# Post-norm transformer layer on one core: five shared places for probabilities, products with V in fewer and longer blocks, one more step of the softmax sums on TensorE

## What is computed

```python
qkv = encodings @ W_attn + b_attn
scores = jnp.einsum('bhki,bhqi->bhkq', k, q) / math.sqrt(HEAD)
scores = jnp.where(mask, scores, jnp.float32(-10000.0))
attn = jax.nn.softmax(scores, axis=2)
combined = jnp.einsum('bhkq,bhkl->bhql', attn, v)
x = _layernorm(x + out @ W_out + b_out)
top_scores, top_idx = jax.lax.top_k(hidden_states @ w_router, k)
h = jax.nn.gelu(selected @ W1 + b1); processed = h @ W2 + b2
x = _layernorm(x.at[top_idx].add(sigmoid(top_scores) * processed))
```

## Time and profile before

| | |
|---|---|
| median of 3 runs (lowest, highest) | 2496.51 us (2496.45, 2498.16) |
| profiled execution, its own time | 2497.64 us |
| its span | 2495.8 us |
| mean granted TensorE clock | 0.993 |
| PE busy | 2437.9 us (98%) |
| POOL busy | 1566.2 us (63%), nearly all of it in the attention part |

### The profile page before, as it was taken

One profiled execution on the slowest core, in us unless ns is written; L12 is line 12 of the kernel. 1 busy time (PEld: TensorE's weight loads), 2 busy tenths in 40 slices (PEclk: granted clock), 3 DMA queues, 4 the chain that ended last, 5 costly groups with the idle time before them and its releaser, 6 DMA issues.

```text
span 2495.8 us, 40908 instructions
## 1 busy us (share of the span) xinstructions
PE 2437.9 (98%) x14104; PEld 1798.0 (72%) x14104; DVE 1677.7 (67%) x4384; ACT 1227.0 (49%) x2211; POOL 1566.2 (63%) x1481
## 2 busy tenths in 40 slices
PE   8999999999999999999999999998999999999997
PEld 6666676777677767676767667763788888888886
DVE  6767778778777777777888787775755544553533
ACT  3665566666566666666666666666531111111110
POOL 2877888788877888877888888885323132221311
PEclk9999999999999999999999999998999999999999
DMA  4233445335344444534434354343421011010100
GB/s 178 95 128 117 161 138 199 129 124 187 136 146 162 145 145 141 175 133 166 157 129 161 125 180 145 128 162 97 169 64 43 19 34 33 26 34 26 32 20 17
DMA packets 167649, 287.72 MB, mean 115 GB/s; under 512 B 23258, under 2 KB 58138, under 8 KB 166172
## 3 DMA queue, kind: packets, MB, share of 16 engines
q1 hardware_dynamic: 160276, 268.26, 31.1%
q0 software_dynamic: 7168, 16.85, 2.1%
HBM read 117.23 MB, written 65.11 MB: 73 GB/s over the span
## 4 chain that ended last, share of the span: by engine, by line
PE 83%; POOL 11%; DVE 2%; issue 1%; ACT 1%; DMA 0%; SPq 0%; POOLq 0%; DVEq 0%; ACTq 0%
PE PS L1623 14%; PE PS L1602 14%; PE PS L1464 11%; POOL Pa L902 10%; PE PS L1549 10%; PE PS L1515 9%; PE PS L1567 9%; PE PS L1472 8%; PE PS L1477 6%; PE PS L1484 2%; POOL Pm L858 1%; PE PS L1439 1%; PE PS L1583 0%; DVE nm L1130 0%; DVE xTl L1223 0%
## 5 line engine op out<-in xcount | busy, mean ns | idle before, releaser
L902 POOL TENSOR_TENSOR Pa<-Pa,Pm 128x512 f32<-128x512 f32 (+1 forms) x602 | 751.9, 1271 | 129.3 <-ACT Pm L1012 106.7
L1549 PE MATMUL PS<-Qp,Kp 128*128 128x512 f32 (+3 forms) x1536 | 491.0, 355 | 8.7 <-ACT Pm L1012 4.1
L1515 PE MATMUL PS<-Kp,Qp 128*128 128x512 f32 (+3 forms) x1536 | 485.3, 351 | 6.6 <-DVE nm L1130 5.5
L1012 ACT ACTIVATE Pm<-PS 128x512 f32<-128x512 f32 (+1 forms) x643 | 358.3, 568 | 243.7 <-PE PS L1549 194.0
L1130 DVE TENSOR_REDUCE nm<-PS 128x1 f32<-128x512 f32 x512 | 344.7, 687 | 157.2 <-PE PS L1515 156.9
L902 POOL TENSOR_TENSOR Pa<-Pa,P 128x512 f32<-128x512 f32 (+1 forms) x297 | 371.9, 1274 | 64.7 <-ACT P L1012 53.6
L1515 PEld LDWEIGHTS PS<-Kp,Qp 128*128 128x128 f32 x1536 | 276.2, 189 | 105.4 <-issue 41.6
L974 ACT ACTIVATE G<-PS,b1c 128x512 f32<-128x512 f32 x128 | 88.2, 689 | 536.5 <-PE PS L1602 520.3
L1549 PEld LDWEIGHTS PS<-Qp,Kp 128*128 128x128 f32 x1536 | 274.8, 189 | 93.5 <-ACT Pa L1012 29.0
L1138 DVE CUSTOM_DVE_ANT_0 PS<-PS,maskA 128x384 f32<-128x384 f32 (+3 forms) x512 | 246.3, 509 | 121.9 <-PE PS L1515 119.9
L1623 PE MATMUL PS<-W2h,Gs 128*128 128x512 f32 x1024 | 316.6, 390 | 1.1 <-DVE W2l L1228 1.1
(11 more groups left out here) (154 smaller groups left out, 4261.2 us busy)
## 6 DMA issues: line engine op xcount, KB each, us to landing
Qp<-nat SPq DMA_DIRECT2D x192, 256.0 KB, 2.5
Kp<-nat SPq DMA_DIRECT2D x192, 256.0 KB, 2.9
o_s<-Of SPq DMA_DIRECT2D x64, 256.0 KB, 2.1
xb<-in_x SPq DMA_DIRECT2D x64, 256.0 KB, 3.4
Ot<-o_s SPq DMA_DIRECT2D x64, 256.0 KB, 3.0
h_s<-hs SPq DMA_DIRECT2D x64, 256.0 KB, 2.1
out<-xb SPq DMA_DIRECT2D x64, 256.0 KB, 2.2
x_raw<-in_xt SPq DMA_DIRECT2D x15, 1024.0 KB, 6.4
```

The lines of the kernel that those rows point to most:

```text
L902: e.tensor_tensor(to, to, probs(u, k)[:, h0:h0 + many, 0:w], ALU.add).then_inc(s["padd"], many)
L1012: e.activation(probs(u, k)[:, hh[0]:hh[-1] + 1, 0:w], tile_bank(j)[:, 0:len(hh) * w].rearrange("p (h n) -> p h n", n=w), ACT.Exp).then_inc ...
L1515: ins = e.matmul(to, Qp[:, u % 4, h_, qt * P:qt * P + P], Kp[:, (2 * i + k0 // 512) % 4, h_, 0:w], start=True, stop=True)
L1549: ins = e.matmul(tile_bank(j)[:, x_ * w:x_ * w + w], Kp[:, (2 * i + k // 4) % 4, h_, k % 4 * P:k % 4 * P + P], Qp[:, u % 4, h_, 512 - w:51 ...
```

## The change

It does four things.

1. The steps of a unit are multiplied with V in fewer blocks: the even unit's four steps in one, the odd unit's eight in 0-1, 2-3 and 4-7.
2. N of the even unit stands behind the odd unit's block 0-1, N of the odd one behind its block 4-7, in the same run of 32-column matmuls. F then stands alone between 128-column matmuls.
3. The last two steps of an odd unit (256 and 128 wide) are summed on PE; POOL makes two additions (of two heads each) less in each of 31 odd units.
4. All five buffers of probabilities (a to e) are one set whose roles turn from pair to pair. The place of a step says which step's reader the exponential waits for. The order of POOL's `keep` and additions comes from a small planner (`sums`) with a cost for each.

```diff
-PRODUCTS = (((0,), (1, 2, 3)), ((0,), (1, 2), (3, 4), (5, 6, 7)))
-PV_LAG = ((1, 2), (2, 2, 3, 3))
+PRODUCTS = (((0, 1, 2, 3),), ((0, 1), (2, 3), (4, 5, 6, 7)))
+PV_LAG = 2
+IN_SUMS = 2
+PLACES = "abccdebcaebb"
+TURN = {"a": "c", "b": "a", "c": "e", "d": "d", "e": "b"}
+KEEP_BEATS, ADD_BEATS, EXP_BEATS = 0.39, {512: 0.78, 384: 0.62, 256: 0.78, 128: 0.78}, 0.6
...
-    return u % 2 == 1 and k == ksteps(u) - 1
+    return u % 2 == 1 and k >= ksteps(u) - IN_SUMS
...
+    steps = [(x_, y_) for x_ in range(max(0, u - 3), u + 1) for y_ in range(ksteps(x_)) if (x_, y_) < (u, k)]
+    last = [x_ for x_ in steps if place_of(*x_) == place_of(u, k)][-1:]
...
-        return 15
+        return 14
...
-                n = self.formed[u, k1] + PV_LAG[u % 2][j]
+                n = self.formed[u, k1] + PV_LAG
+                if u % 2 and j != 1 and not by_products(u):
+                    n = max(n, self.beat["N", u - 1 if j == 0 else u])
...
+    def sums(self):
...
+                if (u, k) not in keeps:
+                    at_add = max(self.formed[u, k] + EXP_BEATS, self.multiplied[u, 0] + 1)
+            t = max(t, min(at_keep, at_add))
+            if at_keep <= t:
+                self.adding.setdefault(int(t), []).append((keeps.pop(0), None))
+                t += KEEP_BEATS
+            else:
+                self.adding.setdefault(int(t), []).append(((u, k), h0))
+                pieces.pop(0)
+                t += ADD_BEATS[width(u, k)]
...
                         e.wait_ge(s["padd"], 4 * additions(a))
                         if k == 1:
                             e.wait_ge(s["pv"], ksteps_before(u) + 1)
...
+                        for u0, k0 in occupants(u, k):
+                            if by_products(u0) and k0 < ksteps(u0) - 1:
...
+                        for k_ in range(ksteps(u)):
+                            if in_sums(u, k_):
+                                ins = sums(u, k_)
...
-                todo += [(1, 2, x_) for x_ in T.pieces[n] if x_[0][0] == "N"]
+                todo += [(3, 2, x_) for x_ in T.pieces[n] if x_[0][0] == "N"]
```

More of the change, by code:

```diff
@@ L98, in in_sums, with place_of, occupants, many_heads @@
 def in_sums(u, k):
-    return u % 2 == 1 and k == ksteps(u) - 1
+    return u % 2 == 1 and k >= ksteps(u) - IN_SUMS
 def additions(a):
-    return a - a // 10
+    return (10 - IN_SUMS) * (a // 10) + min(a % 10, 10 - IN_SUMS)
+def place_of(u, k):
+    name = PLACES[4 * (u % 2) + k]
+    for _ in range(u // 2):
+        name = TURN[name]
+    return name
+def occupants(u, k):
+    if k == ksteps(u) - 1:
+        return []
+    steps = [(x_, y_) for x_ in range(max(0, u - 3), u + 1) for y_ in range(ksteps(x_)) if (x_, y_) < (u, k)]
+    last = [x_ for x_ in steps if place_of(*x_) == place_of(u, k)][-1:]
+    return [x_ for x_ in steps if last and x_[0] == last[0][0] and place_of(*x_) == place_of(u, k)
+            and (x_ == last[0] or x_[1] == last[0][1] - 1 == ksteps(x_[0]) - 2)]
+def many_heads(w):
+    return 1 if w > 256 else 2 if w > P else HG
 def by_products(u):
@@ L206, in __init__ @@
         self.streams()
+        self.sums()
         self.nat, self.packs, self.freed = {}, {}, {}
@@ L251, in streams @@
     def streams(self):
-        self.tiles, self.formed, self.products = {}, {}, {}
+        self.tiles, self.formed, self.products, self.multiplied = {}, {}, {}, {}
         ring = []
@@ L283, in streams @@
             self.ring_no[x[:3]] = j
+    def sums(self):
+        self.adding = {}
+        keeps = [(u, k) for u in range(U) for k in range(ksteps(u)) if diag(u, k) is not None]
+        pieces = [(u, k, h0) for u in range(U) for k in range(1, ksteps(u)) if not by_products(u) and not in_sums(u, k)
+                  for h0 in range(0, HG, many_heads(width(u, k)))]
+        t = float(self.first)
+        while keeps or pieces:
+            at_keep = self.formed[keeps[0]] + EXP_BEATS + (2 if keeps[0][1] == 0 else 0) if keeps else 1e9
+            at_add = 1e9
+            if pieces:
+                u, k, h0 = pieces[0]
+                if (u, k) not in keeps:
[8 more added lines that the diff above has]
+                t += ADD_BEATS[width(u, k)]
     def vector_in(self, n):
@@ L880, in gpsimd @@
                         layer_norm(o_number(j))
-                for u, k in T.steps_formed(n):
-                    i = diag(u, k)
-                    if i is not None and not kept_early(u, k):
+                for (u, k), h0 in T.adding.get(n, ()):
+                    if h0 is None:
                         keep(u, k)
[L885 to L888, removed]
+                        continue
+                    a, w = added(u, k), width(u, k)
+                    if h0 == 0:
+                        if diag(u, k) is not None:
+                            e.wait_ge(s["keep"], diag(u, k) + 1)
                         else:
@@ L893, in gpsimd @@
                             e.wait_ge(s["pv"], ksteps_before(u) + 1)
[L894 to L903, removed]
+                    many = many_heads(w)
+                    to = probs(u, 0)[:, h0:h0 + many, 512 - w:512]
+                    e.tensor_tensor(to, to, probs(u, k)[:, h0:h0 + many, 0:w], ALU.add).then_inc(s["padd"], many)
                 for j in o_add.get(n, ()):
```

34 lines of the change are left out of this document (11 added, 23 removed).

## The result

The changed kernel takes 2621.85 us (median of 4 executions, 2619.41 to 2623.04), the kernel before 2496.73 (2496.45 to 2498.16): a ratio of 1.0496, 95% interval 1.0484 to 1.0509, or 125 us slower. The prediction was 2574, in a range of 2500 to 2625.

The account below looks back on a forecast made before the run. PE's own work was taken as the bound, with waits for POOL coming in. 49 us (middle) + 3 (first pairs) + 25 (clock) = 77 on the profiled 2497.64, which stands 1.13 above the median: 2574 us, range 2500 to 2625.

Parts of the forecast that it names:

- The mechanism: At the odd unit's S step of 512, PE waits for POOL's late-started additions in every pair; chance 0.62.
- The size of the wait in the middle: PE waits for POOL from f + 23.4 to f + 25.5, 2.1 us in every pair; mean 2.4 us.
- None of the four `keep` is late: In POOL's odd-unit chain, exponentials of step 5 are over by about f + 11.4; their `keep` comes at f + 11.2.
- 2.1 - 0.22 = +1.9: Middle pairs without DVE's split: a 2.1 us wait for POOL, less 0.22 us of PE's own work.
- The first pairs: First four pairs, without output projection: both kernels wait for POOL, PE's part is 5 us shorter; +3 us (0 to +8).
- The end: The last unit pair, summed without POOL, was left at zero, give or take 5 us.
- The clock: Waits of PE lower the clock in half of the 30 pairs: 15 x 1.7 = 25 us, ends 0 and 50.
- PE's own work: On PE, 62 fewer blocks save 20.5 us, S steps of 256 cost 13.5: -7 us, -0.22 a pair.
- F alone: F standing alone 62 times on PE, not heading a block: difference taken as zero (-3 to +3 us).
- counting mode changes: By the skill's drain rule on PE, lone F counts too: nothing of 20.5 us saved, work grows by 13.5; prediction rejected it.
- The other waits: Exponentials on ACT wait for readers of shared places: costed at nothing, at most 8 us.
- The old waits: PE's waits of 0.31 and 0.59 us in one pair of four go: about 0.3 us a pair.

Follow-up runs that it names:

- fifth experiment: Changed kernel with N of the odd unit back behind F and the two 384 tiles, V steps 4 to 7 in their own block ahead of F: 2602.95 us.
- third experiment: Changed kernel with each `keep` of POOL planned 0.8 beat later: 2595.53 us.
- the filler: Changed kernel with nine dummy matmuls of 512 ahead of PE's wait at N of the odd unit, from unit 5 on: 2615.7 us.
- second experiment: Changed kernel with the last three steps of each odd unit summed on PE, not two (`IN_SUMS = 3`): 2538.82 us.
- last experiment: Kernel before with the five turning places alone, POOL's order and everything else as before: 2497.52 us.
- seventh experiment: Kernel before with only the odd unit's S step of 256 summed on PE too: 2500.61 us.
- the eleventh and the twelfth kernel: Kernel before with turning places and planner, bias additions at the change's beats: 2505.69 us; with turning places alone, POOL's order as before: 2497.52 us.

## Why the prediction was right in direction and short by 48 us

**The mechanism: right.** V step 0 in the block ahead of F makes POOL start late, and PE waits at the S step of 512. The runs pulled at both ends of the wait: V step 0 earlier gives 86 us, a shorter chain 83, and a chain 0.70 us shorter 0.69 in the half where it stands. It also holds that N's own place hardly matters ("The period is POOL's chain plus PE's way from N to the next V step 0"): the fifth experiment shows it, and in its expectation I had forgotten my own sentence.

**The size of the wait in the middle: short by some 20 us.** With f for the time of the even unit's F, as in the prediction: start, forecast f - 2.4, measured f - 2.24. The additions end: forecast f + 25.5, measured f + 26.31. N could have gone out at f + 23.4 by the forecast, at f + 23.78 by the trace (1078.41 less the wait of 2.59). So the wait is 2.59 and not 2.1. The failed term is "None of the four `keep` is late": two are, by 0.93 and 0.54 us, and without those gaps the chain is 0.70 us shorter (third experiment). I had laid out PE's order by hand for the exponentials of these steps, and PE reaches their B tiles later than that (ACT waits there for most of them, up to 1.53 us). The pairs without DVE's split stood in the sum at 2.1 - 0.22 = +1.9 and came out at +2.7: 0.5 is the wait, 0.3 PE's own part (such a pair takes 52.79 us without its wait, and took 52.70 before). That is 16 us in 20 pairs; the pairs with the split came out as forecast (+2.0), and 4 us are those named above.

**The first pairs: wrong, some 16 us.** "Both kernels wait for POOL there" was a claim that no row bore, and of the kernel before it is true for 2.6 us only. PE's waits for POOL at N in the first four of these pairs, before and after:

```profile
PE PS L1484 <- POOL Pa L902: 2.6, 4, 0.7
```

```profile
PE PS L1519 <- POOL Pa L944: 16.3, 4, 4.3
```

Before, POOL started early enough that 0.7 us was the longest wait. With the late start a PE whose way is 5 us shorter waits all the longer, some 4 us a pair. Of the +28.5 up to the eleventh F some 9 are the clock, 14 this wait, and 5 are PE's waits for DVE's maxima (9.8 us, before 4.7), where I took 3 in all without the clock.

**The end: wrong, some 9 us.** I left it "at zero, give or take 5". Most of it isn't the pair summed without POOL but the last chain with it: some 7 of the 9 us lie in the half of that chain. POOL's timeline after, at the last odd unit that POOL sums (its F at 1786.4):

```profile
1788.36 0.19 POOL L915 TENSOR_SCALAR lnrs<-lnmv 128x1 f32<-128x1 f32 x1 [7.31 <-DVE lnmv L1373]
...
1789.95 5.02 POOL L944 TENSOR_TENSOR Pa<-Pa 128x512 f32<-128x512 f32 x4
```

and before (its F at 1673.7):

```profile
1668.38 10.83 POOL L902 TENSOR_TENSOR Pa<-Pa,Pm 128x512 f32<-128x512 f32 x8 [3.98 <-ACT Pm L1012]
1679.30 0.19 POOL L867 TENSOR_SCALAR lnrs<-lnmv 128x1 f32<-128x1 f32 x1
```

The chain's new place is behind a layer norm's scalars, and those wait for DVE. It starts 3.5 us after F, not 5.3 ahead of it, and PE waits 6.15 us. What is queued ahead of a moved instruction must be looked up at the ends of the program too, where the pattern of the middle doesn't hold.

**The clock: right in sum.** Forecast 15 falls of 1.7, 25 us. There were 21 more than before, and the filler shows 1.3 us for one (one profile of each): 27 us, 14 of them in the middle. The share of the middle's waits with a fall was near the forecast half: 10 of the 25 waits for POOL had one, and the eleventh fall stands behind the 3.35 us for DVE. The Trainium skill (TensorE: Matmul & The Clock Gate, Why this matters for your kernels) ties the loss to gaps longer than these waits; the row at 909.12 disagrees, the one at 1078.41 doesn't.

In all: 21 + 16 + 9 + 2 for the clock are the 48 us. That the range still holds the time, by 3 us, is luck in part: the room in it was meant for the clock, which came as forecast, while the first pairs (19 for 0 to 8) and the end (9 for 5 at most) left their own bounds.

**PE's own work: nearly right, with two terms off that nearly cancel.** In the second experiment, where PE hardly waits, pairs without DVE's split take 53.30 us from F to F where the ones before take 52.74. Two S steps more (0.43 and 0.65) and the 0.31 below would make +1.39, and it is +0.56: two blocks fewer and two lone F give back 0.83 us where I had 0.66. F alone costs next to nothing: it goes out at 1052.04 and the next matmul at 1052.07. By the Trainium skill (TensorEngine Tiling (Array Packing), Key Properties) each change of mode drains TensorE; the trace shows 0.1 us at either end of a run of 32-column steps and next to nothing for this 16-column transpose, so counting mode changes would have been wrong here, as the prediction held.
Against it stands a wait that I hadn't seen. With N ahead of the two 384 tiles, ACT does N's logarithm and exponential first and the exponentials of those tiles later. ACT's timeline after, then PE's:

```profile
1137.16 0.58 ACT L1082 ACTIVATE PS<-PS 128x512 f32<-128x512 f32 x1 [3.71 <-PE PS L1474]
1137.78 0.58 ACT L1084 ACTIVATE PS<-PS 128x512 f32<-128x512 f32 x1
1138.27 0.87 ACT L1047 ACTIVATE P<-PS 128x384 f32<-128x384 f32 x2
```

```profile
1137.98 0.68 PE L1499 MATMUL PS<-xTh,Wkh 128*128 128x512 f32 x2
1138.81 0.44 PE L1585 MATMUL PS<-Qp,Kp 128*128 128x384 f32 x1
```

and before, where the 384 tiles come first:

```profile
1005.47 0.97 ACT L1012 ACTIVATE Pm<-PS 128x384 f32<-128x384 f32 x2
1007.31 0.58 ACT L1047 ACTIVATE PS<-PS 128x512 f32<-128x512 f32 x1 [0.86 <-PE PS L1439]
```

```profile
1008.53 0.68 PE L1464 MATMUL PS<-xTh,Wkh 128*128 128x512 f32 x2
1009.04 0.33 PE L1549 MATMUL PS<-Qp,Kp 128*128 128x384 f32 x1
```

The next B tile on PE goes out 0.82 us behind the first of the two K matmuls ahead of it, before 0.51: 0.31 us late in nearly every pair, some 8 us in the middle. (The expectation of the fifth experiment has 0.42 for it.) With N behind those tiles again (fifth experiment) it is 0.52.

**The other waits: right.** Five turning places: 0.0 us (last experiment). The old waits of the earlier trace rows and the S step: +3.6 (seventh experiment), where the prediction's terms, 13.5 and -0.3 in each of 26 pairs, make +5.7.

**What stays open.** With V step 0 early, 39 us remain over the kernel before (34 in its profile). By the starts of F 6 of them lie ahead of the eleventh; in the middle normal pairs take 0.4 us more (8 us, PE's own work as above with one block more), pairs with DVE's split of x 2.0 us more (12 us: 29.1 and 27.2 for the halves, against 27.04 and 27.37), and some 8 us more in single halves (31.67, 29.42 and 29.37 are the longest). PE's waits say where most of this lies: not at POOL but at DVE. With V step 0 early, in the whole run:

```profile
PE PS L1551 <- DVE nm L1173: 11.8, 16, 3.1
PE PS L1512 <- DVE Os L1364: 10.2, 20, 1.6
```

and before:

```profile
PE PS L1515 <- DVE nm L1138: 0.9, 1, 0.9
PE PS L1477 <- DVE Os L1329: 1.6, 4, 1.0
```

In a half with the split PE waits 0.6 to 1.7 us for DVE's maxima and 0.2 to 0.8 for its `Os`, and the half of 31.67 us holds one wait of 3.10. Why DVE is late there no run shows. Moving the bias additions didn't mend the split pairs, and the last 8 us between the eleventh and the twelfth kernel weren't taken apart.

No version beat the kernel before; the turning places alone equal it.

## What to carry to other kernels

When a step is moved to save the price of a block, ask who starts on its result: POOL's chain of 28 us hung on V step 0, and the move cost 86 us where the saved blocks of the whole change give some 26 (0.83 in each of 31 pairs). The time lost is the helper's chain plus the way from its reader to its next starter, less the main engine's own way; work that sum out at every stage, also where the main engine has less to do, for there the wait is longest. And when a planner writes a helper's order anew, look at what else stands in its queue: two additions of 1.3 us, one within the chain and one right behind it, were worth 27 us, and a layer norm ahead of the last chain goes with a wait of 6.

## What the hardware showed that I had not expected

- Equal waits of 2.59 us on PE ended once with the clock at 1.00 and once at 0.50 for 3.41 us. A fall cost about 1.3 us of the time, less than the 1.7 that half speed takes from 3.41 us, since part of the stretch lies in the wait itself (PE's wait ended at 909.63, 0.51 us into it).
- A lone 16-column transpose between full matmuls took 0.03 us to the next matmul.
